# Attention in a four-layer kernel: unsplit probabilities and values, fp32 products in four column groups, division during the image steps

## What is computed

```python
qkv = x.reshape(B, N, C) @ qkv_w + qkv_b              # B = 16 images, N = 196 tokens, C = 192
q, k, v = ...                                         # 12 heads of 16
attn = einsum('bqd,bkd->bqk', q * scale, k)
attn = attn + (rel_h[..., :, None] + rel_w[..., None, :]).reshape(B * nh, N, N)
attn = softmax(attn, axis=-1)
out = einsum('bqk,bkd->bqd', attn, v)                 # per head
return out.reshape(B, H, W, C) @ proj_w + proj_b
```

## Time and profile before

| | |
|---|---|
| median of three runs | 1793.58 us |
| profiled execution, span from first to last instruction | 1796.6 us |
| l1 image steps, window 642 to 910 | 268 us |
| l3 image steps, window 1485 to 1745 | 260 us |
| PE busy over the span | 1485.9 us (83%) |
| DVE | 1269.7 us (71%) |
| ACT | 973.4 us (54%) |
| POOL | 855.0 us (48%) |
| mean granted clock of PE | 0.802 of 2.4 GHz |

### The profile page before, as it was taken

One profiled execution on the slowest core, in us unless ns is written; L12 is line 12 of the kernel. 1 busy time (PEld: TensorE's weight loads), 2 busy tenths in 40 slices (PEclk: granted clock), 3 DMA queues, 4 the chain that ended last, 5 costly groups with the idle time before them and its releaser, 6 DMA issues. The chain is left out here.

```text
span 1796.6 us, 51708 instructions
## 1 busy us (share of the span) xinstructions
PE 1485.9 (83%) x19315; PEld 1272.1 (71%) x19315; DVE 1269.7 (71%) x4444; ACT 973.4 (54%) x1990; POOL 855.0 (48%) x1080
## 2 busy tenths in 40 slices
PE   4868888888876888889977999899998697888978
PEld 4757777777765776767755667678774586777766
DVE  7877787877778567879956684544446646888974
ACT  3633333333344567889924234555543556888972
POOL 2712222222235056879952111456551416787984
PEclk9955555555558889999986589899995798999998
DMA  3000000000002596667215204322225468666712
GB/s 87 1 20 4 4 5 4 4 4 4 4 3 83 171 257 151 147 156 161 58 48 173 98 24 151 125 81 86 83 73 153 144 159 254 166 147 150 146 29 58
DMA packets 72178, 165.21 MB, mean 92 GB/s; under 512 B 17938, under 2 KB 43162, under 8 KB 69436
## 3 DMA queue, kind: packets, MB, share of 16 engines
q1 hardware_dynamic: 66556, 149.05, 31.3%
q0 software_dynamic: 5376, 12.85, 2.3%
HBM read 93.84 MB, written 67.42 MB: 90 GB/s over the span
## 5 line engine op out<-in xcount | busy, mean ns | idle before, releaser
L1080 POOL TENSOR_TENSOR l_arena<-l_arena,l_arena 98x784 fp32r<-98x784 f32 x192 | 358.4, 1872 | 91.3 <-ACT l_arena L1328 79.0
L514 PE MATMUL gru_ps_r<-gru_hp,gru_wp 128*128 128x16 f16 x3920 | 200.1, 176 | 68.1 <-DVE gru_hp L489 68.1
L514 PEld LDWEIGHTS gru_ps_r<-gru_hp,gru_wp 128*128 128x128 f16 x3920 | 150.8, 106 | 88.5 <-DVE gru_hp L489 88.5
L567 POOL TENSOR_TENSOR gru_kept<-gru_keep,l0s_state 128x32 f32<-128x32 f32 x196 | 49.3, 251 | 305.4 <-ACT gru_keep L582 305.4
L1388 DVE TENSOR_REDUCE l_ps<-l_ps 98x4 f32<-98x784 f32 x192 | 187.5, 977 | 9.1 <-PE l_ps L1159 3.2
L514 PE MATMUL gru_ps_n<-gru_hp,gru_wp 128*128 128x16 f16 x3920 | 191.1, 174 | 0.0
L1197 PE MATMUL l_ps<-l_arena,l_arena 128*66 128x196 f32 x768 | 162.1, 264 | 20.9 <-POOL l_arena L1080 20.1
L580 ACT ACTIVATE gru_reset<-gru_ps_r,gru_unscale 128x32 f32<-128x32 f32 x196 | 56.4, 288 | 216.8 <-PE gru_ps_r L514 216.8
L1325 ACT ACTIVATE l_arena<-l_ps 98x784 fp32r<-98x784 f32 x192 | 158.4, 825 | 4.6
L1328 ACT ACTIVATE l_arena<-l_ps 98x784 f32<-98x784 f32 x192 | 157.0, 818 | 0.0
L1198 PE MATMUL l_ps<-l_arena,l_arena 128*66 128x196 f32 x768 | 155.0, 255 | 0.0
(11 more groups left out here) (389 smaller groups left out, 4568.9 us busy)
## 6 DMA issues: line engine op xcount, KB each, us to landing
l_arena<-qk SPq DMA_DIRECT2D x96, 294.0 KB
qk<-l_arena SPq DMA_DIRECT2D x48, 392.0 KB, 9.0
rel<-l_arena SPq DMA_DIRECT2D x24, 686.0 KB
l_arena<-rel SPq DMA_DIRECT2D x48, 343.0 KB
qk<-l_arena SPq DMA_DIRECT2D x12, 784.0 KB, 7.9
l_arena<-in_experts_dram SPq DMA_DIRECT2D x8, 1152.0 KB, 7.6
l_arena<-x SPq DMA_DIRECT2D x24, 294.0 KB, 5.3
l_arena<-x SPq DMA_DIRECT2D x24, 196.0 KB, 3.1
```

What stands on the lines that cost most here:

```text
L514: last = pe.matmul(out[:, b, B * m:B * m + B], wp[:, wi, g, m, :], hp[:, b, part, B * k:B * k + B], start=False, stop=True, skip_group_che ...
L1080: pool.tensor_tensor(pl[g % LOWS][:TH, :, :], p32[:TH, g % 2, :, :], ph[:TH, g % 4, :, :].bitcast(f32), ALU.subtract).then_inc(pl_ready, 1)
```

## The change

- The probabilities are kept once, as fp32 (`p32`, four slots), and the values once, as fp32, with a column of ones behind each head's 16 (VW = 17). `ph`, `pl`, the value split on POOL and the pads are gone. LAG becomes 3.
- `weigh_values(n)` runs every second step and takes two images. Its 8 products (2 halves of the keys x 2 images x 2 heads) are of type fp32 with 17 weight columns; image and head j = 0 to 3 go to PSUM partitions 32j to 32j + 16, so to four groups of 32 columns of the array. DVE clears that PSUM bank once, and copies all 128 partitions once per two images.
- Sums, reciprocals and their spreading go in eighths of the layer's products (8 images of a pair, 12 in all, h = 0 to 11), by DMA during the image steps. POOL multiplies 128 x 784 by the spread reciprocals, and four DMAs pack each into two full tiles `o_full` of 128 and 64 rows.
- The projection is 2 x 2 fp32 products per tile, without splits; `pick`, its load and the split of the projection's weights are gone.

```diff
-    LAG = 4
+    LAG = 3
-                    dve.tensor_copy(o_quad[p // 2][row:row + 64, b * T:(b + 1) * T], ps[:64, O_BANK, :T]).then_inc(o_kept, 1)
...
-                    dve.tensor_copy(ring[:, slot, b % 2 * T:b % 2 * T + T], ps[64:66, O_BANK, :T]).then_inc(sums_kept, 1)
+                    dve.tensor_copy(o_stage[p][:, c * T:(c + 1) * T], ps[:, O_BANK, :T]).then_inc(o_kept, 1)
```

```diff
-                    for head in range(2):
-                        for keys in range(2):
-                            cols = slice(keys * T, keys * T + T)
-                            values = vs[:, 2 * (g % 8) + keys, head, :]
-                            pe.matmul(out, values, ph[:, g % 4, head, cols], start=head == 0 and keys == 0, stop=False)
-                            last = pe.matmul(out, values, pl[g % LOWS][:, head, cols], start=False, stop=head == 1 and keys == 1)
+                    pe.wait_ge(p_ready, 2 * n + 2)
+                    if n >= 1:
+                        pe.wait_ge(o_kept, n)
+                    for keys in range(2):
+                        for j in range(4):
+                            e, head = divmod(j, 2)
+                            out = ps[32 * j:32 * j + VW, O_BANK, :T]
+                            values = v[:TH, 2 * (2 * c + e) + keys, 2 * p + head, :]
+                            last = pe.matmul(out, values, p32[:TH, (2 * n + e) % 4, head, keys * T:keys * T + T], start=keys == 0, stop=keys == 1)
                     last.then_inc(o_summed, 1)
```

```diff
-                        act.activation(ph[:TH, g % 4, :, :], banks, ACT.Exp).then_inc(p_high, 1)
-                        if g >= 2:
-                            act.wait_ge(pl_ready, g - 1)
-                        act.activation(p32[:TH, g % 2, :, :], banks, ACT.Exp).then_inc(p_ready, 1)
+                        act.activation(p32[:TH, g % 4, :, :], banks, ACT.Exp).then_inc(p_ready, 1)
```

The new DMAs on SP and the new work of POOL (the calls of `store_sums` to `load_spread` lie at steps 8h + 11, + 13, + 17 and + 19, those of `pack` at 8h + 23 or later; those of the last eighths behind the loop):

```diff
+                def store_sums(h):
+                    sp.wait_ge(o_kept, 4 * h + 4)
+                    sp.dma_start(sums_dram[h].rearrange("(j n) -> j n", j=4), o_stage[h // 2][HD:128:32, h % 2 * EIGHT:(h % 2 + 1) * EIGHT]).then_inc(sums_stored, 16)
...
+                def load_spread(h):
+                    sp.wait_ge(rec_stored, 16 * (h + 1))
...
+                    for j in range(4):
+                        row = rec_dram[h].rearrange("(j n) -> j n", j=4)[j:j + 1, :].to_broadcast([HD, EIGHT])
+                        sp.dma_start(spread[32 * j:32 * j + HD, h % 2, :], row).then_inc(spread_in[h % 2], 16)
+
+                def pack(h):
...
+                    sp.wait_ge(divided, h + 1)
+                    for j in range(4):
...
+                        sp.dma_start(place, eighth(h)[32 * j:32 * j + HD, :].rearrange("r (c t) -> r c t", c=4)).then_inc(packed[half], 16)
...
+                for h in range(2 * PAIRS):
+                    o = o_stage[h // 2][:, h % 2 * EIGHT:(h % 2 + 1) * EIGHT]
+                    pool.wait_ge(spread_in[h % 2], 64 * (h // 2 + 1))
+                    pool.wait_ge(o_kept, 4 * h + 4)
+                    pool.wait_ge(sums_stored, 16 * (h + 1))
+                    pool.tensor_tensor(o, o, spread[:, h % 2, :], ALU.mult).then_inc(divided, 1)
```

The projection on PE:

```diff
-                        product3(pe, ps[:CP, 4 + 2 * (n % 2) + m, :TB], lambda c: woh[:, c, m, :], lambda c: wol[:, c, m, :],
-                                 lambda c: oh[:, n % 3, c, :], lambda c: ol[:, n % 3, c, :], blocks=QUADS).then_inc(y_summed, 1)
+                        out = ps[:CP, 2 * (n % 2) + m, :TB]
+                        pe.matmul(out, wo[:, 0, m, :], o_full[0][:, cols], start=True, stop=False)
+                        pe.matmul(out, wo[:64, 1, m, :], o_full[1][:64, cols], start=False, stop=True).then_inc(y_summed, 1)
```

More of the change, by code:

```diff
@@ L738, in weights @@
         at, parts = AT_W, []
-        for dims in ((QUADS, CB, 128), (CB, C), (QUADS, CB, CP)):
+        for dims in ((QUADS, CB, 128), (CB, C)):
             for part in range(2):
@@ L947, in store_reciprocals @@
[L947 to L953 removed]
+                    sp.wait_ge(rec_ready, h + 1)
@@ L973, in main_step @@
                         sp.dma_start(xy[:CP, :, cols], x_in[:, :, cols]).then_inc(x_in_again, 16)
-                    g = i - LAG - 1
-                    if g >= 0 and g % 2 == 1:
-                        store_sums(g)
-                    if i >= 14 and i % 8 == 6:
-                        load_sums((i - 14) // 8)
-                    if i >= 21 and i % 8 == 5:
-                        store_reciprocals((i - 21) // 8)
+                    for at, act_on in ((11, store_sums), (13, load_sums), (17, store_reciprocals), (19, load_spread)):
+                        if i >= at and (i - at) % 8 == 0 and (i - at) // 8 < 2 * PAIRS - 1:
+                            act_on((i - at) // 8)
+                    if i >= 54:
+                        for h in range(2 * PAIRS - 1):
+                            if i == max(8 * h + 23, 54 + 2 * h):
+                                pack(h)
                 for half in range(2):
@@ L994, in _ @@
                     main_step(i)
-                store_reciprocals(2 * PAIRS - 2)
-                load_sums(2 * PAIRS - 1)
-                sp.wait_ge(t_summed, IMAGES)
-                load_spread(0)
-                store_reciprocals(2 * PAIRS - 1)
-                load_spread(1)
+                pack(2 * PAIRS - 2)
+                last = 2 * PAIRS - 1
+                store_sums(last)
+                load_sums(last)
+                store_reciprocals(last)
+                load_spread(last)
+                pack(last)
                 for place, source in extra:
@@ L1064, in _ @@
-                pool.wait_ge(v_ready, 2 * B)
-                pool.memset(ph[CP:, :, :, :].bitcast(f32), 0.0).then_inc(ph_padded, 1)
-                pool.wait_ge(ph_padded, 1)
-                for low in pl:
-                    pool.memset(low[CP:, :, :].bitcast(f32), 0.0).then_inc(pl_padded, 1)
-                pool.wait_ge(pl_padded, LOWS)
-                for n in range(2):
-                    high, low = split_values(n)
-                    for head in range(2):
-                        high(head)
-                    for head in range(2):
-                        low(head)
@@ L1076, in _ @@
-                for g in range(IMAGES):
-                    pool.wait_ge(p_ready, g + 1)
-                    if g >= LOWS:
-                        pool.wait_ge(o_summed, g - LOWS + 1)
-                    pool.tensor_tensor(pl[g % LOWS][:TH, :, :], p32[:TH, g % 2, :, :], ph[:TH, g % 4, :, :].bitcast(f32),
-                                       ALU.subtract).then_inc(pl_ready, 1)
-                    if 5 <= g < IMAGES - 4 and g % 4:
-                        n = (g + 3) // 4
-                        high, low = split_values(n)
-                        if g % 4 == 1:
-                            pool.wait_ge(o_summed, 4 * n - 4)
-                            high(0)
-                        if g % 4 == 2:
-                            high(1)
-                            low(0)
-                        if g % 4 == 3:
-                            low(1)
-                    if g >= 17 and g % 8 == 1:
-                        split_reciprocals((g - 17) // 8)
@@ L1095, in _ @@
[L1095 to L1101 removed]
+                pool.wait_ge(v_ready, 2 * B)
+                pool.memset(v[:TH, :, :, HD:], 1.0).then_inc(ones_ready, 1)
@@ L1300, in constants @@
                     act.activation(ones_at[:TH, :], ident[:TH, :], ACT.Copy).then_inc(ident_ready, 1)
-                    act.wait_ge(pick_in, 16)
-                    act.activation(pick[:, :, :], pick_raw[:, :, :], ACT.Copy).then_inc(pick_ready, 1)
                 if ahead is None:
@@ L2309, in selectors @@
     ident[:TH] = np.eye(TH)
-    pick = np.zeros((2 * HEADS, QUADS, 4, 32), np.float32)
-    for head in range(HEADS):
-        pick[[head, HEADS + head], head // 4, head % 4] = 1.0
-    return np.ascontiguousarray(np.concatenate([sel, ident], 1)), pick.reshape(2 * HEADS, QUADS, 128)
+    return np.ascontiguousarray(np.concatenate([sel, ident], 1))
 def lay_out_attention(tag, wqkv, bqkv, wo, bo, rel_h, rel_w):
```

249 lines of the change are left out of this document (80 added, 169 removed).

## The result

The changed kernel takes 1809.0 us (median of 13 runs) against 1792.7 of the kernel before: ratio 1.0088, 95% interval 1.0067 to 1.0109. It is 0.9% slower, where 1767 us were forecast. The profiled execution has a span of 1809.9 us against 1796.6.

The account below looks back on a forecast made before the run. It took a PE, DVE, PE chain of 2.08 us to close plain steps. Steps +13, drain -5, layer ends -34, other -1 make -27 on 1796.6: 1769.6, less 3 for the runs' median, 1767 us; range 1722 to 1886.

Parts of the forecast that it names:

- The ends: From a layer's last value product through division, packing and projection: 32.8 us against 50.1, -17 a layer, -34 both.
- the sign: Whole kernel: the change was forecast to make it faster, by 27 us; chance of faster 0.61, same 0.05, slower 0.34.
- the start at half clock: Projection at a layer's end: 2 us added for starting at half clock, the rest priced at full clock.
- clock and ends: Rival for the layer ends: PE stays at 1.2 GHz there; +3 us in all, 1797 us, no change; chance 0.12.
- W: Time of the eight fp32 value products of two images on PE: 9 x 0.163 = 1.47 us; break-even at 1.75.
- the rival: Value products in the image steps: all four column groups overlap, 0.65 us, every plain step 2.08; 1697 us, chance 0.15.
- The loops: The 96 image steps of each layer: +7 us a layer, +13 for both.
- Full overlap: Value products of all four column groups at once: -52 us for both layers' image steps; 1697 us in all, chance 0.15.
- late quarter loads: SP's extra DMAs in the image steps: costed at nothing; lateness would show as PE waiting, up to some 5 us.
- the ring: Plain image steps: the chain PE, DVE, PE from logits to next logits, untouched by the change, 2.08 us alone.
- Drain: From a layer's last reduction to its last value product: 9.4 us becomes about 6.7, -2.7 a layer, -5 both.
- Cover: Image steps: the gain of ACT and POOL is hidden, while PE's longer products are not hidden by anything.

Follow-up runs that it names:

- e11b_full32: Changed kernel with the projection's second block over all 128 rows (rows 64 to 127 zero) instead of 64, run four times; 1757.9 us, 0.9808 of the kernel before.
- e8_serial: Changed kernel with all four value products of two images in one column group, same 32 rows, which changes what is computed; 1913.8 us.
- e4_order: Changed kernel with the value products ordered by column group instead of by block of keys; 1807.7 us (kernel before: 1797.5).
- e2_late: Changed kernel with the reciprocals of the sums, and their store, spread and packing, four steps later; 1793.5 us, 1.0004 of the kernel before.
- c6_best1: Changed kernel with late reciprocals (tenth by four steps, eleventh by two, its packing issued earlier) and the projection's second block over 128 rows; 1742.0 us, 0.973 of the kernel before.
- the seven kernels with the same loops: Seven follow-up kernels that leave the step loops as the changed kernel has them; their two loops took 502.1 to 509.7 us together.

## Why the prediction was wrong

**The ends failed, and with them the sign.** The step reads: 8 passes of 392 x 2 / 2.4 GHz = 0.327, 20.9 us for eight tiles, after "2 (the start at half clock)". The pass itself was right: 0.329 us in e11b_full32, where 37.1 us pass from the last value product to the end of the span, against the 32.8 forecast. What was wrong is the 2 us. In the changed kernel's order of 128 and 64 rows the clock stayed at half for the whole projection, 20.9 us a layer in place of the 2, and the gaps at the changes cost 64 x 0.12 = 7.8 us more, which had no term at all. The first tile came at +9.7 and +7.6 instead of +4.4. In the first layer that is 5.3 us: the reciprocals were ready 3.2 us before the last value product instead of 4.5, their store took 3.4 us instead of 1.5, the spreading 3.4 instead of 2.7, the packing 4.2 instead of 2.7. With these each layer comes to 63 to 65 us. The rival "clock and ends" (1797 us, 0.12) had the clock at 0.50 and priced the ends at -4 for both layers. That price is a slip: by the prediction's own terms, 4.4 + 8 x 5.2 + 0.6 + 4.9 = 51.5 us, against 50.1 and 50.8 before, it is +2. From there to the +26 measured, the gaps are 16 us and the later start 9. That a busy TensorE can stand at 0.50 was in the rows that the prediction had the earlier trace rows, and got too little weight: the forecast took the rise from the kernel before, whose projection has 128 rows in all its products.

The Trainium skill, "TensorE: Matmul & The Clock Gate", Part 1, says that sustained matmul activity releases the throttle. By that rule alone the projection, in which TensorE never pauses, would come to full clock. The traces disagree: 44 of 44 us busy at 0.50 with mixed rows and 42 us gapless at 0.50 with 64 rows. The measurement decides.

**W failed, in the cheap direction.** The step "the second pass waits for the first, and whatever follows waits in order" gave 1.47 us. In order holds within a column group only (e8_serial, 0.166 us from pass to pass), not across them (e4_order): the four groups overlap fully, 0.65 us of passes, 0.86 to 1.0 us from the first start to the last end. A plain step is therefore 2.08 throughout, as the rival had it. The Trainium skill, "TensorE: Matmul & The Clock Gate", Part 3, says that products in different column groups run concurrently, which the prediction set aside; the trace agrees. Its other half, that they start and end in program order, does not fit e4_order: issued group by group, 16 passes that start in order would need some 13 rounds, 2.1 us, and they took 1.00.

**The loops came out near the forecast by luck.** The change in them lies between -4 and +8 us over both layers (+7.6 in the profiled execution), against +13. Two errors cancel. Full overlap should have given -52; what took its place shows in the changed kernel's own trace, by steps and for both layers. Steps 23 to 32 and 55 to 62, the reciprocal's wait for its sums and the half-clock steps behind it, took 26 us more than at 2.08 each, and steps 63 to 94, with smaller waits of the same kind, 7 more. Steps 11 and 12, the stall of the relative terms, took 8.7 us more than before instead of somewhat less. The rest lies in the table steps, short ones 2.8 us in the mean against 2.40 and long ones 3.6 against 3.46, and in the half-clock steps right behind them. The prediction costed the reciprocal's wait at nothing: it looked at SP's DMAs only as late quarter loads seen by TensorE, not as a wait on DVE in front of the ring's reduction. What moving it gives is less than it occupies: 18 us in e2_late, 24 in c6_best1, against the seven kernels with the same loops. The stall at step 11 gave back 2 to 6 us a layer, and moving it only moved the loss.

**Drain.** It came to -9, as the full-overlap rival had it (-5 with W = 1.47).

**Cover.** The prediction's statement that the gain of ACT and POOL is hidden by the ring was right for the plain steps: with 158 and 437 us less work they fell by 0.14 us, near the 0.11 that the earlier trace rows show for the wait behind DVE's second copy. The table steps fell by 0.4 to 0.5 us each; they also lost work of TensorE and copies of DVE, and no run separates these.

## What to carry to other kernels

Before counting on the full clock after an idle stretch, look at how many rows the first products have: pad them to 128 rows with zeros, or put the full ones together, and compare with products that raised the clock in this very trace. Price fp32 products in four column groups by the longest group: here the order of issue made no difference. And an operation that waits for a DMA costs its wait on the engine where it is queued: keep it out of the order ahead of the step's critical operation, however short it is.

## What the runs showed of the hardware that was not expected

- What TensorE ran decided whether its clock rose from 0.50, not only how busy it was. Passes of 128 rows raised it, fp32 after 4.6 us and one-pass after 3; passes of 64 rows did not in 42 us. In the changed kernel's order of 128 and 64 rows it did not rise in 49.6 us (fp32) or 39.2 us (one-pass), and with the same fp32 passes four and four it rose after 8 us. A clock of 1.0 stayed up under the changed kernel's order.
- Changing between 128 and 64 rows cost 0.08 to 0.09 us a pass around the change at full clock and 0.11 to 0.14 at half.
- An unsplit fp32 product took two passes of two cycles a column: 0.329 us a pass for 392 columns at full clock, 0.653 at half.
- Sixteen fp32 passes in four column groups took 0.86 to 1.0 us at full clock, 2.83 in one group, and the order of issue made no difference.
